# Two gated attention layers on one core: in layer 1 the value products stand in one group behind the score packs, nine products of the feed-forward move between them, and VectorE masks the single-head maxima

## The reference

```python
attn = jnp.einsum('bhtd,bhsd->bhts', q, k)
causal = jnp.triu(jnp.full((T, S), -jnp.inf, attn.dtype), k=1)
attn = jax.nn.softmax(attn + causal, axis=-1)
...
attn = attn[:, :, 0] - lam * attn[:, :, 1]
out = jnp.einsum('bhts,bhsd->bhtd', attn, v)
```

## Time and profile before

| | us |
|---|---|
| runs before: median (lowest, highest) of 3 | 2339.62 (2337.78, 2343.34) |
| profiled execution: its own time | 2333.17 |
| its span, first to last instruction | 2331.4 |
| TensorE busy | 2123.6 |
| VectorE busy | 1381.2 |
| ScalarE busy | 893.0 |
| GpSimd busy | 665.6 |

### The profile page before, as it was taken

One profiled execution on the slowest core, in us unless ns is written; L12 is line 12 of the kernel. 1 busy time (PEld: TensorE's weight loads), 2 busy tenths in 40 slices (PEclk: granted clock), 3 DMA queues, 4 the chain that ended last, 5 costly groups with the idle time before them and its releaser, 6 DMA issues.

```text
span 2331.4 us, 33812 instructions
## 1 busy us (share of the span) xinstructions
PE 2123.6 (91%) x12386; PEld 1435.3 (62%) x12386; DVE 1381.2 (59%) x2705; ACT 893.0 (38%) x1749; POOL 665.6 (29%) x831
## 2 busy tenths in 40 slices
PE   2389999989999999998999999999999999999998
PEld 1247557575666656675575755657556665666656
DVE  3565565656656666655657566565665666665664
ACT  2142452515524353333524245251452425433352
POOL 2332331313313232223313233141331323222331
PEclk7599999999999999999999999999999999999999
DMA  6813423243131532216231352324313253231530
GB/s 204 294 48 99 156 67 105 73 140 104 52 107 62 177 93 78 81 46 181 92 94 52 95 161 68 105 64 141 106 55 102 71 158 101 63 88 55 179 95 14
DMA packets 105604, 240.51 MB, mean 103 GB/s; under 512 B 17048, under 2 KB 27288, under 8 KB 105184
## 3 DMA queue, kind: packets, MB, share of 16 engines
q1 hardware_dynamic: 91184, 194.41, 27.6%
q0 software_dynamic: 14256, 43.94, 6.2%
HBM read 179.67 MB, written 57.82 MB: 102 GB/s over the span
## 4 chain that ended last, share of the span: by engine, by line
PE 69%; DMA 7%; DVE 7%; SPq 4%; ACT 3%; issue 3%; POOL 1%; DVEq 0%; ACTq 0%; POOLq 0%
PE bank L393 19%; PE bank L552 12%; PE bank L473 11%; PE bank L442 9%; PE bank L489 9%; PE bank L446 3%; DMA qring<-mneg 3%; DMA upring<-up_img 3%; PE bank L571 2%; SPq L351 2%; DVE nmax L724 2%; PE bank L499 1%; DMA k_img<-probs 1%; DVE probs L740 1%; ACT probs L630 1%
## 5 line engine op out<-in xcount | busy, mean ns | idle before, releaser
L724 DVE TENSOR_REDUCE nmax<-bank 128x1 f32<-128x512 f32 (+3 forms) x1056 | 651.7, 640 | 328.1 <-PE bank L446 315.2
L393 PE MATMUL bank<-xnT,upring 128*128 128x512 f32 (+1 forms) x2208 | 632.1, 409 | 24.5 <-DMA upring<-up_img 23.8
L630 ACT ACTIVATE probs<-bank 128x512 f32<-128x512 f32 (+1 forms) x864 | 469.0, 559 | 348.7 <-PE bank L473 335.1
L473 PE MATMUL bank<-qring,kring 128*128 128x512 f32 (+1 forms) x1056 | 476.9, 455 | 55.4 <-ACT probs L630 24.5
L442 PE MATMUL bank<-kring,qring 127*128 127x512 f32 (+3 forms) x1536 | 459.7, 352 | 32.9 <-DMA kring<-k_img 25.9
L393 PEld LDWEIGHTS bank<-xnT,upring 128*128 128x128 f32 x2208 | 402.2, 195 | 106.4 <-issue 32.0
L442 PEld LDWEIGHTS bank<-kring,qring 127*128 127x128 f32 x1536 | 271.3, 194 | 111.3 <-DVE nmax L724 52.6
L552 PE MATMUL bank<-wdown,hbuf 128*128 128x256 f32 x1408 | 327.5, 382 | 0.0
L473 PEld LDWEIGHTS bank<-qring,kring 128*128 128x128 f32 x1056 | 206.6, 197 | 190.3 <-ACT probs L630 100.3
L1505 POOL TENSOR_SCALAR_AFFINE_SELECT probs<-probs 128x512 f32<-128x512 f32 x256 | 162.5, 635 | 517.4 <-ACT probs L630 514.9
L552 PEld LDWEIGHTS bank<-wdown,hbuf 128*128 128x128 f32 x1408 | 260.2, 191 | 32.7 <-issue 1.7
(11 more groups left out here) (119 smaller groups left out, 1525.7 us busy)
## 6 DMA issues: line engine op xcount, KB each, us to landing
upring<-up_img SPq DMA_DIRECT2D x176, 512.0 KB, 4.4
q_img<-probs SPq DMA_DIRECT2D x96, 256.0 KB, 3.1
qring<-q_img SPq DMA_DIRECT2D x256, 64.0 KB, 1.9
kring<-k_img SPq DMA_DIRECT2D x64, 256.0 KB, 3.1
qring<-q_img SPq DMA_DIRECT2D x32, 384.0 KB, 4.6
k_img<-probs SPq DMA_DIRECT2D x48, 256.0 KB, 4.6
up_img<-hbuf POOLq DMA_DIRECT2D x22, 512.0 KB, 5.1
gring<-gate_img POOLq DMA_DIRECT2D x32, 256.0 KB, 3.7
```

Source lines behind the costliest of these rows:

```text
L393: last = nc.tensor.matmul(out_ap, part_a(a, pa, k), part_b(b, pb, k), start=(n == 0), stop=(n == len(steps) - 1))
L473: nc.tensor.matmul(SC[n % 2][:, 0:heads * w].rearrange("p (g n) -> p g n", g=heads), kring[l][:, ks, kt * P:(kt + 1) * P], qring[l][:, s, ...
L630: nc.scalar.activation(pr, pr if biased else scores, ACT.Exp, scale=scale).then_inc(s_exp, 1)
L724: nc.vector.tensor_reduce(nmax[:, u % 2, g0:g0 + heads, qt], MX[n % 2][:, 0:heads * w].rearrange("p (g n) -> p g n", g=heads), AX.X, ALU.m ...
```

## The change

In units 4 to 10 (`third_apart`), of which there are 56 in the 8 batches:

- all four value products stand in one group at the unit's end, with the turn of outputs of unit u - 1 ahead of them, and both behind `pe_max_turn`. Four places for exponentials make this possible: kt 2 goes into `xn[0]` (unused in layer 1), kt 3 into the free end of place 1 (in all units);
- 9 of the 12 products of the tile stand inside packs 0 to 8, one each, and 3 behind pack 10;
- on ScalarE the tanh stands behind the exponentials of pack 8, and the copy of maxima behind those of pack 10, where it stood ahead of them;
- `dve_normalise(u - 1)` stands at the end of VectorE's unit instead of behind maximum 4.

For every single-head maximum of layer 1 (8 of 11 packs in each unit), the product with `causal_bf` is gone, and VectorE masks and reduces in one `tensor_tensor_reduce`, which adds a strip of zeros and minus 3e38 in bf16, writes the sums back into the bank and the maximum into `nmax`. Here `nmax` isn't negated in layer 1, and the copy to `mneg` has a scale of -1.

```diff
+        def third_apart(u):
+            return UNITS[0] <= u < U_ALL - 1
+
+        def probs_of(u, kt):
+            if kt == 3:
+                return probs[:, 1, :, 3 * P:T]
+            if kt == 2 and third_apart(u):
+                return xn[0][:]
+            return probs[:, kt % 2, :, 0:T - P * kt]
...
+            if l == 1 and heads == 1:
+                last.then_inc(s_mp[k], 1)
+                return
 
             diag = bk[:, 0:heads * w].rearrange("p (g n) -> p g n", g=heads)[:, :, qt * P:w]
...
+            if l == 1 and heads == 1:
+                scores = MX[n % 2][:, 0:w]
+                nc.vector.tensor_tensor_reduce(scores, scores, mask_strip[:, T - w:T], 1.0, -BIG, ALU.add, ALU.max,
+                                               nmax[:, u % 2, g0, qt:qt + 1]).then_inc(s_mr[k], 1)
+                return
...
-                            pe_up(pe, TILE_AFTER[u], 0, i, 1)
-                        if i == 3 and u not in U0:
+                            pe_up(pe, tile, 0, i, 1)
+                        if at_end and i < UP_INSIDE:
+                            pe_up(pe, tile, i // UP_STEPS, i % UP_STEPS, 1)
+                        if i == 3 and u not in U0 and not at_end:
                             pe_out_turn(pe, u - 1)
-                        if i == (7, 5)[layer_of(u)]:
+                        if i == (7, 5)[layer_of(u)] and not at_end:
                             pe_pv(pe, u, 0)
...
-                    pe_pv(pe, u, 1)
-                    if more:
+                    if at_end:
+                        pe_up(pe, tile, 1, UP_INSIDE - UP_STEPS, 2 * UP_STEPS - UP_INSIDE)
                         pe_max_turn(pe, u + 1)
-                    if u < U_ALL - 1:
-                        pe_up(pe, TILE_AFTER[u], 0)
-                    pe_up(pe, TILE_AFTER[u], 1)
-                    pe_pv(pe, u, 2)
-                    pe_pv(pe, u, 3)
+                        if u not in U0:
+                            pe_out_turn(pe, u - 1)
+                        pe_pv(pe, u, 0)
+                    if not third_apart(u):
+                        if u < UNITS[0]:
+                            pe_pv(pe, u, 1)
+                            if more:
+                                pe_max_turn(pe, u + 1)
+                            pe_up(pe, tile, 0)
+                        pe_up(pe, tile, 1)
+                    for kt in range(2 if u < UNITS[0] else 1, NT):
+                        pe_pv(pe, u, kt)
```

53 lines of the change are left out of this document (36 added, 17 removed).

## The result

The changed kernel takes 2279.01 us (median of 4 runs, 2277.15 to 2289.04) against 2341.46 for the kernel before beside it: a ratio of 0.9746, 95% interval [0.9718, 0.9773]. Measured once more on another occasion it was 2287.51 against 2335.86, 0.9785 [0.9763, 0.9807].

The account below looks back on a forecast made before the run. TensorE's products were taken to bound the kernel, the row of maxima only 0.28 us behind. Units 5 to 10 would gain 0.26 us each and unit 4 lose 0.38: 9.4 us over 8 batches, forecast 2329 us, range 2300 to 2352.

Parts of the forecast that it names:

- part (a): From a unit's first score product to its last: 7.33 us before, forecast at 7.35, between 7.1 and 7.65.
- the nine products: Nine products of the tile moved in between the packs: 0.2425 us each, 2.18 us added.
- The causal products: Eight causal products taken out of a unit's packs: 0.72 us saved, between 0.46 and 0.92.
- The tenth taken off for changes between kinds of products: 0.1 us off the packs' sum: no normalisation between VectorE's maxima, fewer changes between kinds of products on TensorE.
- VectorE inside (a): In the packs, a masked single-head maximum takes about 0.80 us (0.67 for 384 columns); nothing added to the packs' time.
- Rival 2: VectorE's masked maximum bounds the packs: with pairs at 0.95 and 0.82 us, about 2365 us; chance 0.15.
- Part (b): From a unit's last score product to the next unit's first: 5.89 us before, 5.61 forecast, row of maxima ending last.
- The term of 2.6 for the landing: At a unit's end, the row of maxima lands 2.6 us after its issue, median of 96, taken as unchanged.
- Rival 1: Packs shrink more, causal products worth 0.115 us each, first to last score product 7.1 or below: 2310 to 2316; chance 0.20.
- Rival 3: At a unit's end the row lands later, with 512 KB of weights starting behind it: 40 us lost, 2380; chance 0.09.
- rival 4: Nothing gained: first to last score product 7.6 us, idle time before the row takes the rest, 2335 to 2344; chance 0.18.
- Edits at nothing: Moved tanh, normalisation and tile load, unit 4's maxima, and exponentials freed in layer 0 and unit 11: counted as nothing.

Follow-up runs that it names:

- moves_only: The changed kernel with causal products and plain maxima put back in every pack, all moves kept: 2333.54 us, ratio 0.9989.
- inside_0: The changed kernel with none of the tile's products between the packs, three ahead of the turn of maxima and nine behind it: 2321.81 us, ratio 0.9914.
- tile_later: The changed kernel, but from unit 5 on SyncE issues the later tile's load only after 4 score packs of the unit: 2286.13 us, ratio 0.9787.
- masks_only: The kernel before with only the masked single-head maxima and without their causal products, order otherwise as before: 2338.52 us, ratio 1.0.
- moves_0: moves_only with none of the tile's products between the packs, three ahead of the turn of maxima and nine behind it: 2319.33 us, ratio 0.9925.
- keys_first: The changed kernel with the 256 KB load of keys issued ahead of the four loads of queries, row of maxima still last: 2266.73 us, ratio 0.9683.
- after_again: The changed kernel, unaltered, measured and profiled once more on another occasion: 2287.51 us, ratio 0.9785.
- keep_warm: The changed kernel with twelve products that nothing reads added behind unit 4's last value product: 2283.49 us, ratio 0.9757.
- warm_6: The changed kernel with six of the tile's products inside the packs and keep_warm's twelve unread products: 2280.08 us, ratio 0.975.

## Why the prediction was wrong

**The step that failed** is the sum for part (a), and under it the sentence that "TensorE has no idle time to win there". 7.35 was forecast, 6.69 came. By the terms: the nine products were priced at 2.18, as if the packs around them were full. With causal products in place, moves_only has (a) at 7.53 where these terms give 7.33 - 0.36 - 0.99 + 2.18 = 8.16: 0.63 us less. The causal products were worth 0.84 (7.53 - 6.69) for 0.72, well inside their bounds. The tenth taken off for changes between kinds of products was not found. 0.63 + 0.12 - 0.10 = 0.65 is the miss of 0.66.

**Why the term was wrong.** The packs of before were held again and again by a maximum or an exponential that had not yet given its bank back, and TensorE stood in gaps between its products that the windows view books as busy, because the modelled end of a product covers them. One such place in the unit of the earlier trace rows:

```profile
303.98 2.65 DVE L724 TENSOR_REDUCE nmax<-bank 128x1 f32<-128x512 f32 x4 [0.85 <-PE bank L446]
...
304.35 0.47 PE L473 MATMUL bank<-qring,kring 128*128 128x512 f32 x1
304.73 0.50 PE L442 MATMUL bank<-kring,qring 127*128 127x512 f32 x1
```

The max product of pack 2 writes the bank that the first of the four reductions reads until 304.67, and starts at 304.73, 0.38 us behind its score product (in packs 0 and 1 it is 0.31 and 0.32). Bare packs take 6.27 to 6.29, with or without causal products. Work put between them is nearly free until it has filled the gaps, and causal products taken out save nothing until then. That is why the halves are worth nothing apart and 2.5% together. The trace of before could have shown it. Unit 4 has no turn of outputs in its packs, and its (a) is 7.30 against 7.35: I took the turn at 0.36, from 305.74 to 306.10, and wrote 6.97 for unit 4 without reading its own rows. And the pack distance of 0.60 that I used isn't that of all: the first three in units 6 to 9 of before are 0.61, 0.60 and 0.76 us apart. Equal work at unequal distances is the mark of somebody else's pace.

**VectorE inside (a).** The instructions take 0.70 and 0.57 us, priced at 0.69 and 0.56: right. The accumulator's read takes 142 ns for 120, but next to nothing is added by it: in the profile after, pairs follow each other every 0.69 and 0.59 us, not 0.80 and 0.67, and even that is TensorE's pace. In inside_0, where VectorE holds seven products in each unit, pairs of 512 columns start 0.65 us apart in the median and 0.61 at the least, plain reductions 0.61. Rival 2 rested on the sum of the two, so the sign of its premise was right (VectorE is near the bound, and holds packs again with six products inside) and its price wrong.

**Part (b).** 5.61 was forecast and 5.47 to 6.08 came in units 6 to 9. The sign and the mechanism hold: TensorE idle ahead of most units, row as releaser, 50 times where "over 40" was said. The term of 2.6 for the landing was a median over 96 rows of different kinds: amid the loads of a later unit it is 2.89 in the mean, without them (unit 10) 1.8, and in front of unit 5 4.2. The trace of before had this too, with 2.80, 1.8 and 3.8. Why the row of unit 5 is so late was not followed. Unit 10, which was to be like the others, has a (b) 1.08 us shorter than before, 4.83, where TensorE's own work ends last. That work was forecast at 5.19. Unit 4 as a whole went from 13.98 to 14.34 (medians; the means 14.22 and 14.30) where 0.38 more was forecast, though by other terms: 0.51 less in (a), 0.73 more in (b).

**The rivals.** Rival 1 pointed the right way, with (a) at "7.1 or below", but for causal products worth 0.92 in all. They were worth 0.84, which is only 0.12 more than the forecast had and explains that much of the 0.66. Even its price, 2300 to 2316, missed. Rival 3 fell with tile_later, rival 4 with the result. No case had the kernel below 2300, because none asked what a product between the packs costs when TensorE isn't the one that paces them.

**Edits at nothing.** Unit 5's (a) of 8.09 is a cost that no term had: the wait ahead of it is followed by a lower clock. It takes 9 us (7.79 in the mean for 6.69, eight batches). On the other side the stages outside units 4 to 10 gave some 1.1 us a batch, 9 us, so the two cancel. From the first score product of unit 1 to that of unit 3, 33.84 became 33.58, with moves_only at 33.59 and masks_only at 33.86, so that part belongs to the moves; why was not followed. The rest differs between the runs by as much as was gained, so it isn't shown to come from the change.

## What to carry to other kernels

Before a product is priced at its distance in a run of its own kind, find out who paces the place it goes into: compare two units that differ by one piece of work (unit 4 and unit 5 here), compare the distances of equal packs, or see whether a product starts right when another engine has given its bank back. A busy share of TensorE doesn't answer that, and neither does an idle VectorE: it waited for TensorE in the same packs of before in which it held TensorE (0.18, 0.44 and 0.24 us in the unit of the earlier trace rows). And when a unit waits for a small load, list all loads that start with it and their landings: here the largest, issued first, was worth more than the small one issued earlier.

## What the runs showed of the hardware

- A masked maximum is a main instruction of 701 ns (512 columns) or 569 ns (384) and an accumulator read of 142 ns, and the next main instruction can start together with the read (292.04, 292.04 in masks_only); the pairs of 512 columns that nothing holds start 0.61 to 0.65 us apart (inside_0), plain reductions 0.61. The two-instruction form that the Trainium skill's "VectorE: DVE Perf Modes" describes (section "Two Vector instructions with no wait between them") is in the trace; its price is not the sum of both. With the result written into the bank, the main instruction takes 701 ns against 687 for the plain reduction.
- A causal product of 128 columns costs 0.105 us in a full stream (moves_only against the changed kernel), 0.01 in the packs of before (masks_only) and nothing in bare packs that VectorE and ScalarE hold (inside_0, moves_0).
- The row of 8 KB lands in 1.8 us where no load of a later unit is ahead of it, 2.4 with the keys first and the queries right ahead of it, 2.9 behind queries and keys, and 3.3 when it starts from another queue 0.4 earlier amid the same loads. Its end is tied to theirs: 0.2 us behind the last of them in the mean, in after and in keys_first.
- The granted clock went to 0.50 (1.2 GHz) behind the wait in front of unit 5 in 16 of the 24 batches of after, after_again and keys_first, behind waits from 2.11 to 3.29 us, and stayed at 1.00 in the other eight, behind waits of 2.47 to 3.15. Where TensorE had work in that wait (keep_warm, warm_6) it never fell there, in 16 batches. What tells the batches apart is open.
